# Macaron block on one core: key sums and value products in one run, maxima transposed behind it

## The reference

```python
x = x + 0.5 * ffn(layernorm(x))        # ffn: layernorm * gamma + beta, ternary 512x512 weight, bias
x = x + attention(layernorm(x))        # 16 heads of 32 channels, rotary q and k, block mask
x = x + 0.5 * ffn(layernorm(x))

scores = einsum('bhqd,bhkd->bhqk', q, k) * SCALE      # SCALE = 32 ** -0.5
scores = where(mask, scores, -inf)                    # causal by blocks of 64 keys
attn   = softmax(scores, axis=-1)
ctx    = einsum('bhqk,bhkd->bhqd', attn, v)
out    = ctx @ w_o.T
```

## Time and profile before

| | us |
|---|---|
| median of 3 runs | 645.0 (644.71 to 647.46) |
| profiled execution, device time | 645.08 |
| its span in the profile | 643.3 |
| PE busy | 575.6 |
| DVE busy | 400.7 |
| ACT busy | 318.4 |
| POOL busy | 239.6 |

### The profile page before, as it was taken

How to read it: one execution, slowest core, us unless ns; L and a number is a source line. 1 busy time by engine, 2 the same in 40 slices (tenths; PEclk the granted TensorE clock), 3 DMA queues, 4 the chain that set the end, 5 groups by cost and what they waited for, 6 DMA issues and landing times.

```text
span 643.3 us, 10070 instructions
## 1 busy us (share of the span) xinstructions
PE 575.6 (89%) x3586; PEld 219.8 (34%) x3586; DVE 400.7 (62%) x782; ACT 318.4 (49%) x629; POOL 239.6 (37%) x200
## 2 busy tenths in 40 slices
PE   0483899869969999999999999999999999999876
PEld 0432545424423233233233233233333223333432
DVE  5999515616877667667667667667657842331572
ACT  1731722312226656656656656657645548572421
POOL 1511053563656547546546546546600100000100
PEclk9995889998979999999999999999999999999997
DMA  9921013550322125322223115415310003100011
GB/s 321 337 76 65 1 50 115 180 158 25 100 74 75 51 76 172 116 66 95 73 59 122 51 51 164 149 50 162 118 51 2 2 0 132 50 18 34 34 66 65
DMA packets 43553, 57.95 MB, mean 90 GB/s; under 512 B 3478, under 2 KB 34326, under 8 KB 42480
## 3 DMA queue, kind: packets, MB, share of 16 engines
q1 hardware_dynamic: 42924, 57.21, 26.7%
q10 hardware_dynamic: 580, 0.11, 0.1%
HBM read 32.01 MB, written 25.17 MB: 89 GB/s over the span
## 4 chain that ended last, share of the span: by engine, by line
PE 77%; DVE 13%; ACT 5%; issue 3%; DMA 2%; POOL 0%; SPq 0%; ACTq 0%; DVEq 0%
PE bank L901 13%; PE bank L944 12%; PE bank L1043 11%; PE bank L1033 11%; PE bank L927 10%; PE bank L855 6%; PE bank L981 5%; PE bank L865 5%; DVE stats L654 3%; ACT big L541 2%; DMA rows<-in_L_attn_x_dram 2%; DVE big L669 2%; PE bank L845 2%; DVE rmax L796 1%; ACT xh L540 1%
## 5 line engine op out<-in xcount | busy, mean ns | idle before, releaser
L796 DVE TENSOR_REDUCE rmax<-bank 128x1 f32<-128x512 f32 (+3 forms) x384 | 202.7, 553 | 128.0 <-PE bank L927 123.8
L606 ACT ACTIVATE big<-bank 128x512 f32<-128x512 f32 (+3 forms) x384 | 182.2, 490 | 151.4 <-PE bank L901 146.9
L927 PE MATMUL bank<-kst,qst 104*128 104x512 f16 (+3 forms) x384 | 126.2, 331 | 13.2 <-issue 10.2
L901 PE MATMUL bank<-qst,kst 106*128 106x512 f16 (+3 forms) x384 | 126.6, 331 | 1.6 <-ACT big L606 1.6
L499 POOL TENSOR_TENSOR rot<-t,sin_s 64x512 f32<-64x512 f32 x64 | 81.7, 1276 | 117.5 <-ACT t L599 114.9
L901 PEld LDWEIGHTS bank<-qst,kst 106*128 106x128 f16 x384 | 36.7, 96 | 137.5 <-ACT big L606 74.2
L1043 PE MATMUL bank<-big,rows 128*32 128x512 f32 (+3 forms) x768 | 81.8, 498 | 0.0
L1033 PE MATMUL bank<-big,ones 128*32 128x512 f32 (+3 forms) x768 | 81.8, 498 | 0.0
L508 POOL TENSOR_TENSOR rhl<-t,rhl 128x512 f16<-128x512 f32 x32 | 37.0, 1156 | 62.9 <-ACT rhl L620 62.9
L944 PE MATMUL bank<-xh,wh 128*128 128x512 f16 x128 | 50.0, 391 | 8.9 <-DVE xl L690 6.5
L927 PEld LDWEIGHTS bank<-kst,qst 104*128 104x128 f16 x384 | 37.8, 98 | 44.1 <-issue 14.9
(11 more groups left out here) (106 smaller groups left out, 674.6 us busy)
## 6 DMA issues: line engine op xcount, KB each, us to landing
spread<-rhl SPq DMA_DIRECT2D x32, 256.0 KB, 2.2
qst<-spread SPq DMA_DIRECT2D x16, 384.0 KB, 3.7
kst<-spread SPq DMA_DIRECT2D x16, 384.0 KB, 3.8
rows<-in_L_attn_x_dram SPq DMA_DIRECT2D x4, 1024.0 KB, 12.5
x<-rows SPq DMA_DIRECT2D x4, 1024.0 KB, 4.8
spread<-rhl SPq DMA_DIRECT2D x32, 128.0 KB, 2.1
xh<-ch SPq DMA_DIRECT2D x4, 512.0 KB, 4.2
xl<-cl SPq DMA_DIRECT2D x4, 512.0 KB, 5.4
```

The costliest lines, as they stand in the source:

```text
L606: nc.scalar.activation(probs[:, st % P_PLACES, h, 0:n], pb[u % 2][:, 0:n], ACT.Exp, scale=EXP_SCALE).then_inc(s_eb, 1)
L796: nc.vector.tensor_reduce(rmax[:, at:at + 1], a_bank(u)[:, 0:n], AX.X, ALU.max, negate=True).then_inc(s_max, 1)
L901: nc.tensor.matmul(pb[u % 2][:, 0:n], kst[0:ROWS_B, g % SETS, h, j * P:(j + 1) * P], qst[0:ROWS_B, g % SETS, h, q0:q0 + n], start=True, st ...
L927: nc.tensor.matmul(a_bank(u)[:, 0:n], qst[0:ROWS_A, g % SETS, h, i * P:(i + 1) * P], kst[0:ROWS_A, g % SETS, h, half * HALF:half * HALF + ...
```

## The change

Eight edits, all of them to the order of the work; no instruction is added or removed.

- `B_START` 20 to 18 and `A_START` 11 to 10: both kinds of score unit move to earlier steps against the projections.
- `PV_LAG` 7 to 9: the products of an st now fall into the step in which the sums of the next st are, right behind them on PE.
- `MAX_PLACE` 5 to 2, and the transposed maxima move on PE from the 6th step after a head's last unit, between units B and A, to the 2nd, behind the sums and products. The explicit wait for reductions at that place goes.
- The other engines' parts of the maxima follow: DVE's small rows from the step after the last unit to the same step, ACT's copy from the 7th to the 3rd, SP's DMA from the 8th to the 4th.
- The logarithm is taken in the step of the last sums, four steps ahead of the reciprocal; DVE's scaling, ACT's and POOL's split of the context come one step earlier against the last product.

```diff
-A_START, B_START = 11, 20
-SUM_LAG, PV_LAG = 5, 7
+A_START, B_START = 10, 18
+SUM_LAG, PV_LAG = 5, 9
...
-MAX_PLACE = 5
+MAX_PLACE = 2
...
-                if e := max_head(k, 8):
+                if e := max_head(k, 4):
...
-                if c := ctx_half(k, 5):
+                if c := ctx_half(k, 4):
...
-                if e := max_head(k, 7):
+                if e := max_head(k, 3):
...
-                if c := ctx_half(k, 0):
+                if c := ctx_half(k, -4):
                     n = 2 * c[0] + c[1]
                     act.wait_ge(s_sum, 12 * c[0] + 4 + 8 * c[1])
                     if n:
                         act.wait_ge(s_cl, n)
                     nc.scalar.activation(cf[:, :], psum[:, :], ACT.Ln).then_inc(s_ln, 1)
+                if c := ctx_half(k, 0):
+                    n = 2 * c[0] + c[1]
                     act.wait_ge(s_ln, n + 1)
                     nc.scalar.activation(cf[:, :], cf[:, :], ACT.Exp, scale=-1.0).then_inc(s_rec, 1)
-                if c := ctx_half(k, 4):
+                if c := ctx_half(k, 3):
...
-                if e := max_head(k, 1):
+                if e := max_head(k, 0):
...
-                if c := ctx_half(k, 2):
+                if c := ctx_half(k, 1):
...
-                if e := max_head(k, MAX_PLACE + 1):
-                    n = GH * e[0] + e[1]
-                    pe.wait_ge(s_max, A_UNITS * (n + 1) + (MAX_PLACE - 2 if n + 1 < GH * ALL else 0))
-                    pe.wait_ge(s_mp, n + 1)
-                    nc.tensor.transpose(max_bank(n)[0:2 * TILES, 0:P // 2].bitcast(F16),
-                                        mparts[:, n % 2, :, :].rearrange("p a t -> p (a t)"),
-                                        ident16[:, :]).then_inc(s_mtr, 1)
...
                     last.then_inc(s_pv, 1)
+                if e := max_head(k, MAX_PLACE):
+                    n = GH * e[0] + e[1]
+                    pe.wait_ge(s_mp, n + 1)
+                    nc.tensor.transpose(max_bank(n)[0:2 * TILES, 0:P // 2].bitcast(F16),
+                                        mparts[:, n % 2, :, :].rearrange("p a t -> p (a t)"),
+                                        ident16[:, :]).then_inc(s_mtr, 1)
```

## The result

The kernel after takes 635.1 us (median of 4 runs, 633.35 to 636.03) against 644.9 beside it on the same chip: a ratio of 0.9835, with a 95% interval of 0.9803 to 0.9868. It is faster, by 9.8 us where 15.8 were forecast, inside the range. The profiled execution took 634.88 us, with a span of 633.1; the two profiled executions are 10.2 apart.

A forecast was written before the change was run, and what follows sets the result against it. PE's own instruction order was taken to bound the kernel, busy 400.65 of 403 us in the main stretch. Terms -23.8 - 2.5 + 8.5 + 2.0 = -15.8 took 645.1 to 629.3 us, range 617 to 640.

The forecast's parts named there:

- The likeliest case: Gain from merged runs and transposes less waits at the transposes: 622 to 637 us, chance 0.55.
- Runs merged: Sums and products on PE: 192 runs become 97, saving 95 entries and exits of 0.25 each, 23.8 us.
- The join: Passage from sums to products inside a merged run: taken as costing nothing, with bounds of 0 to 14 us in all.
- The rival of a dear join: Each join inside a merged run costs 0.106 or 0.147, giving 639.4 or 643.3 us; chance 0.15.
- Transposed maxima: Behind the run, 28 heads save a 0.09 entry each, 2.5 us; 2.5 more if run to transpose costs no exit.
- The wait at the transpose: PE waits for DVE's small rows held behind POOL: 7.5 us in six groups plus 1 early, 8.5 in all.
- The dead heat: DVE's L809 and POOL's rotation both due at 1.53 after unit A starts; st 0's wait of 0.5 taken half.
- The first rival: No wait at the transpose, DVE ahead of POOL or the run hiding it: 623.6 us, chance 0.22.
- Starting A earlier: Earlier A and B help little: two early pauses end with the stacks' DMA, 0.65 against 0.65; no gain or loss.
- Burst of scores: Four score steps between runs instead of two: exponentials and reductions keep up, 0.28 slack, no cost.
- logarithm: On ACT in the step of its sums: delays nothing if PE stands until 2.95, otherwise 2.8 us.
- Tail: Behind unit A's end, ACT's 0.60 sets the pace of B's score matmuls: two four-step groups cost 2 us.

The follow-up runs named there:

- e9: Kernel after with POOL's rotation behind DVE's small rows and ACT's split two steps earlier for a group's last projection only: 620.8 us.
- e12: e9 with the merge undone (PV_LAG 7, logarithm two steps ahead of the reciprocal), so sums and products run apart: 641.15 us.
- e3: Kernel after with POOL's rotation made to wait for DVE's small rows of the head: 626.8 us.
- e11: Kernel after with ACT's split copy at lag 6 instead of 8 for a group's last projection only: 630.7 us.
- e7: Kernel after with the transposed maxima behind the following run (MAX_PLACE 6), A still starting at step 10: 630.35 us.
- e2: Kernel after with the merge undone: PV_LAG back to 7, logarithm lag -2, all other moves kept: 645.6 us.
- e10: e1 with unit B two steps earlier (B_START 18), A and transposes as in the kernel before: 640.7 us.
- e1: Kernel before with only the runs merged (PV_LAG 9) and the logarithm two steps ahead of the reciprocal: 646.75 us.
- e5: Kernel after with POOL's rotation behind DVE's small rows and ACT's split two steps earlier at every projection: 643.7 us.
- e8: Kernel after with the logarithm back beside the reciprocal (lag 0), four steps later: 652.3 us.

## Why the prediction was right, and by how much it was off

The likeliest case came about: a gain from merged runs and transposes, part of it given back where the transpose waits for DVE behind POOL. The sum was 5.8 too good in the medians (5.6 against the profiled 634.88). Term by term:

- **Runs merged, -23.8.** Measured with the waits mended (e9 against e12): -20.4 in all. In the steady groups the size was right: twelve joins save 47.70 - 44.84 = 2.86, 0.238 each for the 0.25 that were taken; 95 x 0.238 is 22.6. The join, taken as nothing, costs 0.03, and the exit is as much cheaper, so that 1.85 stands as forecast: the low end of the bounds, 0 to 14. The rest was lost outside: one group of e9 still holds the wait of 1.0 and takes 46.02, and behind the last copy e9 gains 5.0 on e12 (440.67 to 620.4, against 455.01 to 639.7), where some 30 joins would give 7.1. The rival of a dear join is out: its 0.106 or 0.147 would show as 1.96 or 2.00 where 1.85 stands. So the rule of the Trainium skill ("TensorE: Matmul & The Clock Gate", on packing small matmuls), that a load overlaps only with other rows, doesn't hold for these loads, and its sentence on the spare weight buffer does.
- **Transposed maxima, -2.5.** Too small. At the place of before each cost 0.10 on the way in and 0.10 on the way out. Behind a merged run it costs 0.01 in and 0.10 out, and the run's own exit, 0.12 where a run meets unit B, is not paid: 0.21 each, 28 x 0.21 = 5.9. The prediction named this as what might be "2.5 more". No run moves the transposes alone, but e12 comes near: its runs are apart as before, PE waits in neither between 195 and 480, and a group takes 47.70 for 48.64, 0.94 or 0.235 for each of four; there the exit that goes is that of a run alone. It fits the Trainium skill ("TensorEngine Tiling (Array Packing)", Key Properties), by which only a change of the tiling mode drains the array: run and transpose both have weights of at most 32 columns in the rows. That 16 and 32 columns count as one mode is a reading of the 0.01.
- **The wait at the transpose, +8.5.** Right in mechanism and place; e3, which removes the cause alone, takes 8.3 off. The dead heat is lost in every group, not in half: st 0 is 0.55 late (taken as 0.25), st 3 0.85 (0.8), st 9 0.2 (0.2), st 6 not at all. That is 1.6 a group, 9.5 in six. The first four heads lose more than the 1 that was taken: the copy at the start of the steady stretch comes 1.3 later than before (193.99 against 192.68). Together 10.8. That e3 shows 8.3 goes with what it gives back: the wait for the stack grows by 1.1 there, and the same early copy comes at 195.54, 1.5 later. The first rival, no wait, is out, with 1081 ns as L811's mean.
- **Starting A earlier, 0.** This is the step that failed: "Starting A and B earlier helps little", counted as costing nothing too. I looked at the two pauses at the start alone. In the steady stretch the first unit A of a group is a step (0.65) earlier against the projections, and all steps have become shorter, while the chain from the projection to the stack lasts as long as before. It is 4.3 us by e11, the largest part of the error, and the listed waits grow in the faster kernels (5.4 in e3, 5.5 in e7). It takes the faster PE too: e2, which starts A as early but runs sums and products apart, has none of these waits, while e10, which merges with A at its old step, has two short ones (0.5 together). No run parts the two causes cleanly.
- **Burst of scores, 0, and logarithm, 0.** Right here. Between 195 and 480 PE never waits for an exponential. But the cover is real: e1 shows the wait as soon as the gaps lie behind the run, e5 its full price, and e8 that the logarithm in its old company costs 17.
- **Tail, +2.0.** Right in place, not in size. The three waits of unit B for ACT behind 480 are 0.52, 0.44 and 1.21, 2.2 together, but the kernel before had four of 1.2 together there, so 1.0 is new. First the list of before, then the last of the three:

```profile
PE bank L901 <- ACT big L606: 1.2, 4, 0.4
```

```profile
535.75 0.23 PE L903 MATMUL bank<-qst,kst 106*128 106x128 f16 x1 [1.21 <-ACT big L606]
```

The stretch behind the last copy lost more than these waits show. It became 5.2 shorter (453.56 to 633.1, against 458.62 to 643.3), where some 30 joins and six transposes would take off 8.4 at the sizes of the steady groups. So 3.2 are missing, and 2.2 of them stay open.

In a steady group the sizes close: e9, without waits, takes 44.84; with 1.6 at the transposes and 0.9 at the stack that is 47.34, and the kernel after takes 47.33. Over the whole kernel they make -22.6 - 5.9 + 10.8 + 4.3 + 3.2 = -10.2, against -9.8 in the medians and -10.2 between the profiled executions. That it meets to the tenth is luck: the last term is a remainder of its own stretch, and the others are good to some tenths at best. Part of the nearness of the forecast is luck as well: the gain at the transposes was 3.4 better than taken, which covers most of the 4.3 that had been overlooked.

Counted as parts, the edits do not add up: merging gives nothing in the layout of before (+1.7), 10.5 in that of after and 20.4 with the waits mended.

## What to carry to other kernels

Where PE sets the end, a block of work that costs PE time on the way in and out is worth joining, but the joined block leaves longer stretches without it. Here it helped to have the steps with the least work in front of the block (646.75 to 640.7 us from e1 to e10), though that alone did not bring the gain. List, for each engine that used to be paid out of the pauses, what it holds up. When PE gets faster, every fixed chain that feeds it (here copy, rotation, split, two DMAs) comes nearer to being late: price the chain for the next user, not only for the one at the start. Mend such a wait where it occurs, not at each instance of the line that causes it.

## What the runs showed of the hardware beyond what was expected

A merged run of 128 x 32 weights passes into a transpose with 16 weight columns for 0.01 us, and one run into the next for 0.03. Into the full array a merged run passes for 0.12 and a run alone for 0.147, so that the merged run pays the fixed cost of a single one. A DVE instruction that takes 0.17 us alone took 1.08 in the mean of 32 where POOL's two rotations are under way or begin just before it; letting DVE in first gave back 8.3 us. The Trainium skill ("SBUF — State Buffer", on the shared port pair) tells of this lock, and the 168 ns of e3 bear it out from the other side: who is let in first decides, and the loser's followers pay.
